# The selective scan's block below the diagonal by way of the states, with one decay tile for both diagonal blocks

## What is computed

```python
value = silu(v_conv)                                   # (B, 256, 16 heads, 16)
Bm = (xm @ B_proj_w).reshape(Bb, L, HS, NS)            # xm (B, 256, 128), NS = 64
Cm = (xm @ C_proj_w).reshape(Bb, L, HS, NS)
decay = exp(A * dt)                                    # one number per head
# chunks of 64 tokens; inside a chunk:
y_diag = einsum('bchqk,bchkp->bchqp', (C B^T) * decay**(q-k), x_dt)
states = einsum('bchtn,bchtp->bchnp', Bp * decay**(chunk-1-t), x_dt)
y_off  = einsum('bchtn,bchnp->bchtp', Cp, h_carry) * decay**(t+1)
y = (y_diag + y_off) + D_param * value
y = y.reshape(Bb, L, DI) * silu(gate) @ out_proj_w
```

## Time and profile before

| | |
|---|---|
| median of 3 runs | 1000.96 us (999.48 to 1003.15) |
| the profiled execution | 1003.44 us |
| its span, first to last instruction | 1001.7 us |
| TensorE | 926.0 us busy, 92% of the span |
| VectorE | 668.7 us, 67% |
| ScalarE | 647.6 us, 65% |
| GpSimd | 463.9 us, 46% |
| mean granted TensorE clock | 0.991 |

### The profile page before, as it was taken

How to read it: one execution, slowest core, us unless ns; L and a number is a source line. 1 busy time by engine, 2 the same in 40 slices (tenths; PEclk the granted TensorE clock), 3 DMA queues, 4 the chain that set the end, 5 groups by cost and what they waited for, 6 DMA issues and landing times.

```text
span 1001.7 us, 24912 instructions
## 1 busy us (share of the span) xinstructions
PE 926.0 (92%) x9520; PEld 802.7 (80%) x9520; DVE 668.7 (67%) x1962; ACT 647.6 (65%) x1511; POOL 463.9 (46%) x739
## 2 busy tenths in 40 slices
PE   6879989898999999999999999999999999999996
PEld 6768778676978888796978879797988877878896
DVE  5345888987867676867668577767768685753320
ACT  3664636767658576776668577676767678578541
POOL 2385333536263644626265344725354447355432
PEclk9999999999999999999999999999999999999999
DMA  7000000000000000000000000000000000000000
GB/s 275 1 2 7 12 7 2 7 3 11 2 18 1 2 18 6 13 2 17 2 17 2 2 17 2 17 2 17 2 17 2 8 7 11 1 13 12 12 6 6
DMA packets 17204, 14.47 MB, mean 14 GB/s; under 512 B 1856, under 2 KB 15552, under 8 KB 16832
## 3 DMA queue, kind: packets, MB, share of 16 engines
q1 hardware_dynamic: 17088, 12.89, 4.1%
HBM read 10.79 MB, written 2.10 MB: 13 GB/s over the span
## 4 chain that ended last, share of the span: by engine, by line
PE 58%; ACT 14%; DVE 11%; POOL 10%; issue 6%; DMA 0%; SPq 0%; POOLq 0%; ACTq 0%; DVEq 0%
PE bank L1239 54%; DVE M L1030 3%; POOL hD_lo L647 3%; POOL P L577 2%; ACT h L890 2%; POOL hD_lo L642 2%; ACT P L857 2%; PE bank L1250 2%; DVE mneg L1148 1%; ACT h L896 1%; DVE cv L1017 1%; POOL w_h_lo L634 1%; ACT junk L698 1%; ACT LM L692 1%; ACT L890 1%
## 5 line engine op out<-in xcount | busy, mean ns | idle before, releaser
L1030 DVE TENSOR_TENSOR M<-bank,LM 128x384 f32<-128x384 f32 x256 | 126.4, 549 | 69.4 <-PE bank L1239 69.3
L1239 PE MATMUL bank<-hD_hi,w_h_hi 128*128 128x256 f32 x512 | 147.7, 288 | 8.9 <-POOL hD_lo L647 6.5
L1239 PE MATMUL bank<-hD_hi,w_h_lo 128*128 128x256 f32 x512 | 143.6, 280 | 0.0
L1239 PE MATMUL bank<-hD_lo,w_h_hi 128*128 128x256 f32 x512 | 143.5, 280 | 0.0
L1148 DVE TENSOR_REDUCE mneg<-bank 128x2 f32<-128x512 f32 (+1 forms) x192 | 122.1, 683 | 13.7 <-PE bank L1239 13.5
L857 ACT ACTIVATE P<-bank 128x512 f32<-128x512 f32 x192 | 102.7, 611 | 18.2 <-PE bank L1239 18.0
L577 POOL TENSOR_SCALAR_AFFINE_SELECT P<-P 128x256 f32<-128x256 f32 (+1 forms) x192 | 91.5, 495 | 36.8 <-ACT P L857 34.1
L1239 PEld LDWEIGHTS bank<-hD_hi,w_h_hi 128*128 128x128 f32 x512 | 96.5, 188 | 13.8 <-POOL hD_lo L647 9.3
L1239 PE MATMUL bank<-BC 64*128 64x256 f32 (+1 forms) x1024 | 101.5, 337 | 4.8 <-ACT BC L705 3.6
L705 ACT ACTIVATE BC<-bank 128x512 f32<-128x512 f32 x128 | 75.3, 606 | 46.3 <-PE bank L1239 43.7
L896 ACT ACTIVATE h<-bank,cols 128x256 f32<-128x256 f32 x128 | 53.4, 471 | 79.3 <-PE bank L1239 78.9
(11 more groups left out here) (252 smaller groups left out, 2643.4 us busy)
## 6 DMA issues: line engine op xcount, KB each, us to landing
xh<-in_x SPq DMA_DIRECT2D x16, 128.0 KB, 2.1
P<-in_w_h SPq DMA_DIRECT2D x2, 1024.0 KB, 9.0
x_res<-in_x SPq DMA_DIRECT2D x16, 128.0 KB, 2.4
out<-out_sb SPq DMA_DIRECT2D x16, 128.0 KB, 1.9
M<-in_w_B SPq DMA_DIRECT2D x1, 512.0 KB, 3.9
M<-in_w_C SPq DMA_DIRECT2D x1, 512.0 KB, 4.4
Qs<-in_w SPq DMA_DIRECT2D x2, 256.0 KB, 5.3
M<-in_w_in SPq DMA_DIRECT2D x1, 256.0 KB, 3.1
```

Source lines behind the costliest of these rows:

```text
L1030: last = v.tensor_tensor(M[:, k % 2, r, e, :], psum("C", i, 2 * n + e)[:, 0:TRI], LM[:, h + e, :, :].rearrange("p a q -> p (a q)"), ALU.mult)
L1239: return p.matmul(o, lhsT, rhs, start=start, stop=True, skip_group_check=True)
```

## The change

The block below the diagonal is no longer made as a 128 x 128 product for each head. The values of the first tile are scaled by decay^(127-k) (`xw`, on DVE), multiplied by `xm` (`gs`, one fp32 product with 256 columns), copied by ACT (`Gs`), and turned into the states of all heads by eight fp32 products with `w_B` as the stationary operand and 32 columns each (`st`); DVE keeps each head's own part (`Sp`). In `va`, four more products of 128 columns take `Sp` times C of the second tile into a bank of their own; DVE multiplies that by decay^(q+1) (`yo`), and POOL adds it (`yadd`). `LM` keeps one 128 x 128 block per head, which serves both diagonal blocks. `sc` makes eight products of 128 columns for four heads and holds two banks; `mask` becomes one DVE operation of 128 x 512 for two heads and two tiles. `BC` gets eight tiles, so that all C of a unit stay until `va`. `w_B` gets a tile of its own. `TURNS`, `BANKS` and `FILL` are new: 220 identity products, 94 in unit 0, 15 in unit 1, 79 in the last two units, 32 in the units between (54 before). In unit 0 TensorE's order is now `bc` 0, `bc` 1, `sc` 0, `bc` 2, `bc` 3, `sc` 1, `gs`, `bc` 4, `st`, then four items of unit 1; DVE takes `st` ahead of its first two `mask` items, and ACT takes the first `bc` after one of the four groups of exponentials, where it took it after all four.

```diff
-    xm_hi=1, n_hi=1, conv=2 * KC, val=1, cb_full=SCORES, masked=SCORES, y_mm=2, yacc_free=2, yg=2,
+    xm_hi=1, n_hi=1, conv=2 * KC, val=1, xw=1, cb_full=4, masked=8, y_mm=2, yo=2, yacc_free=2, yadd=2, yg=2,
...
-    LM = sb("LM", [P, HS, 3, P])
+    LM = sb("LM", [P, HS, P])
+    DR = sb("DR", [P, HS])
+    DQ = sb("DQ", [P, 2, P])
...
         def yg_(i, b):
+            late = yg[:, b, P:L]
+            pool.wait_ge(S["yo"], at(i, "yo", b + 1))
             pool.wait_ge(S["yacc_free"], at(i, "yacc_free", b + 1))
+            g.tensor_tensor(late, late, yo[:, b, :], ALU.add).then_inc(S["yadd"], 1)
+            pool.wait_ge(S["yadd"], at(i, "yadd", b + 1))
             g.tensor_tensor(yg[:, b, :], yg[:, b, :], gate[:, b, :], ALU.mult).then_inc(S["yg"], 1)
...
             for h in range(4 * k, 4 * k + 4):
-                last = a.activation(LM[:, h, :, :].rearrange("p a q -> p (a q)"), diff, ACT.Exp, scale=sc[:, 3, h:h + 1])
+                last = a.activation(LM[:, h, :], diff, ACT.Exp, scale=sc[:, 3, h:h + 1])
+            if k == 0:
+                a.activation(DR[:], sc[:, 3, 0:HS], ACT.Exp, scale=back)
+                for b in range(2):
+                    last = a.activation(DQ[:, b, :], steps, ACT.Exp, scale=sc[:, 3, HS + b:HS + b + 1])
...
         def bc(i, hp):
-            if SCORES * i + hp >= 4:
-                act.wait_ge(S["cb_full"], at(i, "cb_full", hp - 3))
-            copy("S", i, hp, BC[hp % 4][:].rearrange("p m l -> p (m l)"))
+            if i > 0:
+                act.wait_ge(S["y_mm"], at(i, "y_mm", hp // 4 - 1))
+            copy("S", i, hp, BC[hp][:].rearrange("p m l -> p (m l)"))
+
+        def gs_(i, _):
+            if i > 0:
+                wait_full(act, "M", i - 1, M_ST)
+            copy("M", i, M_GS, Gs[:], psum_t("M", i, M_GS))
...
+        def xw_(i, _):
...
+            v.tensor_tensor(xw[:].rearrange("p (b h c) -> p b h c", b=2, c=PS), first, left, ALU.mult).then_inc(S["xw"], 1)
+
+        def st_(i, _):
...
+            wait_full(dve, "M", i, M_ST)
+            of = psum_t("M", i, M_ST).rearrange("p (n c) -> p n c", c=2 * PS)
+            v.tensor_tensor(Sp[:], of, pairs.unsqueeze(1).to_broadcast([P, SCORES, 2 * PS]), ALU.mult).then_inc(evac("M", M_ST), 1)
...
-            for e in range(2):
-                last = v.tensor_tensor(M[:, k % 2, r, e, :], psum("C", i, 2 * n + e)[:, 0:TRI], LM[:, h + e, :, :].rearrange("p a q -> p (a q)"), ALU.mult)
-            last.then_inc(S["masked"], 1)
...
+            decay = LM[:, h:h + 3:2, :].unsqueeze(2).to_broadcast([P, 2, TILES, P])
+            v.tensor_tensor(M[:, k, e, :, :, :], psum("C", i, n).rearrange("p (n k q) -> p n k q", n=2, q=P), decay, ALU.mult).then_inc(S["masked"], 1)
 
         def yg_(i, b):
             dve.wait_ge(S["y_mm"], at(i, "y_mm", b + 1))
+            if i > 0:
+                dve.wait_ge(S["yadd"], at(i, "yadd", b - 1))
+            v.tensor_tensor(yo[:, b, :], psum("Y", i, 2)[:, b * P:(b + 1) * P], DQ[:, b, :], ALU.mult).then_inc(S["yo"], 1)
...
+        def gs_(i, _):
+            pe.wait_ge(S["xw"], i + 1)
+            wait_free(pe, "M", i, M_GS)
+            mm(psum_t("M", i, M_GS), xm[i % 2][:, 0, :], xw[:], True).then_inc(full("M"), 1)
+
+        def st_(i, _):
+            wait_evac(pe, "M", i, M_GS)
+            wait_free(pe, "M", i, M_ST)
+            for n in range(SCORES):
+                two = slice(2 * PS * n, 2 * PS * (n + 1))
+                last = mm(psum("M", i, M_ST)[:, two], w_B[:, n * P:(n + 1) * P], Gs[:, two], n == 0)
+            last.then_inc(full("M"), 1)
...
-            for n in (2 * k, 2 * k + 1):
-                CB, Bt, Ct = [psum("C", i, 2 * n + e) for e in range(2)], BC[n % 4][:, 0, :], BC[n % 4][:, 1, :]
-                for e in range(2):
-                    r64 = slice(e * NS, (e + 1) * NS)
-                    mm(apart(CB[e][:, 0:TRI]), Bt[r64, 0:P], Ct[r64, 0:L].rearrange("p (a q) -> p a q", q=P), True)
-                for e in range(2):
-                    r64 = slice(e * NS, (e + 1) * NS)
-                    last = mm(CB[e][:, P:L], Bt[r64, P:L], Ct[r64, P:L], False)
-                last.then_inc(S["cb_full"], 1)
+            for e in range(2):
+                wait_free(pe, "C", i, 2 * k + e)
+            for n in range(2):
+                Bt, Ct = [BC[2 * k + n][:, m, :] for m in range(2)]
+                for t in range(TILES):
+                    for e in range(2):
+                        r64, tok, o = slice(e * NS, (e + 1) * NS), slice(t * P, (t + 1) * P), psum("C", i, 2 * k + e)
+                        last = mm(o[:, (TILES * n + t) * P:(TILES * n + t + 1) * P], Bt[r64, tok], Ct[r64, tok], n + t == 0)
+            last.then_inc(S["cb_full"], 1)
...
+            for t in range(TILES):
+                for e in range(2):
+                    for q in range(4):
+                        o = acc[32 * q:32 * q + 32, t * P:(t + 1) * P]
+                        mm(o, xpad[:, t, 8 * b + 2 * q + e, :], M[:, q // 2, e, q % 2, t, :], start=(b + t + e == 0))
+            for q in range(4):
+                last = mm(late[32 * q:32 * q + 32, :], Sp[:, 4 * b + q, :], BC[4 * b + q][:, 1, P:L], start=(b == 0))
```

More of the change, by code:

```diff
@@ L83, in _scan @@
         if k % 2 == 1:
-            items += [("va", k // 2)]
-    return items + [("yg", 1)]
+            items += [("va", k // 2), ("yg", k // 2)]
+    return items
 def _chains():
@@ L185, in _opened @@
     return dict(
-        xm_turn=["M", M_XM], n_turn=["M", M_N], gates=["M", M_G + k], val_turn=["M", M_XT], bc=["S", k], sc=["C"] + [4 * k + h for h in range(4)],
-        va=["Y", 0] if k == 0 else [], m_out=["D", D_O] if k == 0 else [], n2_turn=["D", D_N2], up=["D", D_FC + k],
+        xm_turn=["M", M_XM], n_turn=["M", M_N], gates=["M", M_G + k], val_turn=["M", M_XT], gs=["M", M_GS], st=["M", M_ST], bc=["S", k], sc=["C", 2 * k, 2 * k + 1],
+        va=["Y", 0, 2] if k == 0 else [], m_out=["D", D_O] if k == 0 else [], n2_turn=["D", D_N2], up=["D", D_FC + k],
         down=["Y", 1] if k == 0 else [], n3_turn=["H", H_N3], qkv=["H", H_QKV], qk_turn=["K", K_Q + k], k_turn=["A", A_K],
@@ L230, in program @@
     sl = sb("sl", [P, 512])
-    diff = sl[:, 0:3 * P]
+    diff, steps, back = sl[:, 0:P], sl[:, P:2 * P], sl[:, 2 * P:2 * P + 1]
     sq = sb("sq", [P, TILES, QK, PA])
@@ L293, in program @@
     xpad = sb("xpad", [P, TILES, HS, 2 * PS])
-    BC = [sb(f"BC{b}", [P, 2, L]) for b in range(4)]
-    M = sb("M", [P, 2, 2, 2, TRI])
+    BC = [sb(f"BC{b}", [P, 2, L]) for b in range(SCORES)]
+    M = sb("M", [P, 2, 2, 2, 2, P])
+    xw = sb("xw", [P, DI])
+    Gs = sb("Gs", [P, DI])
+    Sp = sb("Sp", [P, SCORES, 2 * PS])
+    yo = sb("yo", [P, 2, P])
     yg = val
@@ L1334, in va @@
                 wait_evac(pe, "M", i, M_XT)
+                wait_evac(pe, "M", i, M_ST)
                 wait_free(pe, "Y", i, 0)
+                wait_free(pe, "Y", i, 2)
             acc = block(psum("Y", i, 0), b)
+            late = psum("Y", i, 2)[:, b * P:(b + 1) * P]
             pe.wait_ge(S["masked"], at(i, "masked", 4 * b + 4))
-            for k in range(2):
-                for j in range(4):
-                    o = acc[32 * j:32 * j + 32, :].rearrange("p (a q) -> p a q", q=P)
-                    mm(o, xpad[:, 0, 8 * b + 4 * k + j, :], apart(M[:, k, j // 2, j % 2, :]), start=(b + k == 0))
-            for k in range(2):
-                for j in range(4):
-                    last = mm(acc[32 * j:32 * j + 32, P:L], xpad[:, 1, 8 * b + 4 * k + j, :], M[:, k, j // 2, j % 2, P:L], False)
+            for t in range(TILES):
[5 more added lines that the diff above has]
+                last = mm(late[32 * q:32 * q + 32, :], Sp[:, 4 * b + q, :], BC[4 * b + q][:, 1, P:L], start=(b == 0))
             last.then_inc(S["y_mm"], 1)
```

196 lines of the change are left out of this document (99 added, 97 removed).

## The result

The changed kernel takes 1022.8 us (median of 4 runs, 1022.1 to 1024.8) against 1002.0 (999.5 to 1003.2) for the kernel before beside it: a ratio of 1.022, 95% interval 1.020 to 1.024. It is slower by 20.8 us, where 992 was forecast with a range up to 1011. The profiled execution has a span of 1021.2 us against 1001.7.

The account below looks back on a forecast made before the run. TensorE, 96% busy from 250 to 800 us, was taken as the bound: 1003.44 - 1.6 (work) - 4 (start) - 4 (idle later) = 993.8 us profiled, median 991.4, stated as 992, range 975 to 1011.

Parts of the forecast that it names:

- The states cost TensorE what the triangle saves: TensorE's work: columns saved in sc and va are paid back in st's weight loads; sum with fills -1.6 us.
- four terms: TensorE's product changes over the run: sc -28.2 us, va -7.0, gs +7.0, st +29.8.
- Fills: -3.2 us: TensorE's identity products: 220 for 232 at 0.27 us each, counted as 3.2 us less work.
- has fewer holes: Units 1 to 13: fills placed in TensorE's idle time go from 77 to 47, read as a sign of fewer holes.
- The start: -4 us: Start of the run: sc 0 at 33 to 34 us, 3.5 us sooner; net -4 us, bounds 0 and -8.
- the sign named was before 57: Start of the run: val's product by the gate was to come before 57 us; it stood at 59.43.
- whatever else is late there stays: Start of the run: the other causes of TensorE's 20.5 us idle in the first 100 us remain as they were.
- Idle time later: -4 us: TensorE between 100 and 800 us: 4 us of the 12.7 + 23.2 us idle given back, bounds -14 and +8.
- VectorE falls by 30 us: VectorE's busy time: masks from 140 to 87 us, new items add 23; off the path where TensorE is 96% busy.
- `st` lets the clock fall: Rival: each unit's st brings a clock fall of 1.7 us, 27 us in all, 1019 us; chance 0.08.
- the loads of `st` lie bare: Rival: st's weight loads are not covered by streams, +26 us on the sum, 1018 us; chance 0.09.
- even* rival: Rival: work and idle time stay even, the start's gain eaten by its own longer chain; 999 us, chance 0.26.

Follow-up runs that it names:

- experiment 4: Kernel before without the block below the diagonal in sc, masks and va (left out of the output): 975.3 us, ratio 0.975.
- experiment 5: Kernel after without the states (xw, gs, st, Sp, late products, yo, yadd), GpSimd's w_h_lo pieces still long: 982.6 us, ratio 0.983.
- experiment 6: Kernel after without the states (xw, gs, st, Sp, late products, yo, yadd), w_h_lo made in narrow pieces of 128 x 256: 977.5 us, ratio 0.977.
- Experiment 8: Kernel before without the identity products of units 1 to 13 (77 of 232): 1004.0 us, ratio 1.004.
- experiment 1: Kernel after with GpSimd's two w_h_lo subtractions of 128 x 2048 cut into 16 of 128 x 256: 1015.9 us, ratio 1.016.
- experiment 7: Kernel of experiment 1, TensorE reading always-ready tiles in place of xw, Gs and Sp, which are still made: 1013.3 us, ratio 1.013.
- experiment 3: Kernel after with st in one fp32r pass for two, 8 records for 16: 1009.6 us, ratio 1.010.
- experiment 11: Kernel of experiment 1 with GpSimd's 64 hD_lo subtractions replaced by writes of zeros: 1001.7 us, ratio 1.000.

## Why the prediction was wrong

**"The states cost TensorE what the triangle saves"** was right on the products that it priced, and 2.8 us off. From start to start, summed over the run without idle time: `sc` 97.2 to 72.2 us, -25.0 (predicted -28.2); `va` with the late products 46.1 to 39.8, -6.3 (-7.0); `gs` +7.9 (+7.0); `st` +27.8 (+29.8). That is +4.4, where the same four terms made +1.6. The pace taken for `st`, that of a load, was the right one: 1.70 us for 16 records. The term that was mis-sized most is `sc`: its groups take 72.2 / 64 = 1.13 us on average for the 1.08 of the sum. In time the two did not balance: the states cost 38.4 us and the triangle had cost 24.9 (experiments 4 to 6), since TensorE waits more where products are taken out.

**4.1 us more of products** (8.5 - 4.4) belong to no step of the prediction. Some 3 of them are the hidden layer's products (`hD` with `w_h`, 1536 records), which go from 187.6 to 190.7 us, start to start. They rose without the states too (190.6 and 189.2 in experiments 5 and 6), and not in experiment 4 (187.6). Neither the states nor `st` is the cause; what is was not settled.

**"Fills: -3.2 us" is the first step that failed.** It counted fewer identity products as work saved. Experiment 8 shows that they are not such a term: 21.6 us fewer made the kernel 3.5 us slower. The same error stood in the sign that the order "has fewer holes": 47 products for 77 in the middle need not mean fewer waits; without the states the holes are the same in both orders (148.1 and 148.5). Between 250 and 800 us TensorE's busy time fell by 8.6 us while its identity products became fewer.

**"The start: -4 us" is the second.** Its first link was right: `sc` 0 at 33.5 us for 36.95. But by unit 0's `m_out` the gain of 3.4 us was gone or nearly so, at 58.8 us against 60.3, where the sign named was before 57. Without the states the same order has it at 54.4 (experiment 5), so the longer chain of unit 0 costs 4.4 us where the prediction had 1.5; TensorE's idle time in the first 60 us is 15.9 us for 16.8. And "whatever else is late there stays" was taken for granted. What VectorE does between 62 and 72 us was new: the conv of unit 1 now met `w_h_lo`. That cost a wait of 8.2 us on TensorE and 5 to 7 us of time (experiment 1), more than the start had won. Both halves of it could have been read beforehand, in the diff and in the trace: the order of VectorE's items, and two GpSimd operations of 4.6 us with two SBUF inputs. The prediction priced VectorE's items by their quiet durations and never asked what ran beside them.

**"Idle time later: -4 us" is the third.** No such gain came. From 250 to 800 us TensorE is idle for 31.8 us, where it was for 23.2. Without the collision the kernel has holes of 143.7 us against 139.0. Of these 4.7 us, 2.6 are put down to the three hand-overs (experiment 7, within its noise); about 2 stay open. Taking work from TensorE does not by itself close holes, it opens some: without the triangle (experiment 4) products fell by 37.6 us and holes grew by 9.1.

**"VectorE falls by 30 us"** was wrong too, though it is off the path. The row of masks fell as forecast for each, 683 ns for 128 x 512, from 126.4 to 82.8 us in the row:

```profile
L1059 DVE TENSOR_TENSOR M<-bank,LM 128x512 f32<-128x512 f32 x128 | 82.8, 683 | 19.2 <-PE bank L1270 18.8
...
L1029 DVE SCALAR_TENSOR_TENSOR cv<-vpad,cols,cv 128x256 f32<-128x256 f32 x96 | 67.3, 701 | 3.4
...
L1065 DVE TENSOR_TENSOR yo<-bank,DQ 128x128 f32<-128x128 f32 x32 | 8.9, 278 | 13.0 <-PE bank L1270 13.0
L1046 DVE TENSOR_TENSOR Sp<-bank,cols 128x256 f32<-128x256 f32 x16 | 6.8, 425 | 51.1 <-PE bank L1270 51.1
L1039 DVE TENSOR_TENSOR xw<-bank,DR 128x256 f32<-128x256 f32 x16 | 6.7, 421 | 14.7 <-PE bank L1332 13.1 <-ACT DQ L699 1.6
```

The prediction took 256 x 549 = 140 us for the old masks, where overlapping ones are busy for 126.4, and 87 for the new. It had them fall by 53 us, and they fell by 43.6: that is 9 of the 38 us missing. The added items cost what was said, 8.9 + 6.8 + 6.7 = 22.4 us. The `cv` row grew by 17 us, from 50.0 (521 ns each) to 67.3 (701), without one `cv` more: hold-ups by GpSimd. It falls to 60.2 with the narrow pieces and to 51.7 when GpSimd writes zeros for `hD_lo` as well (experiments 1 and 11). The other 12 us are spread over small rows.

**The rivals.** That `st` lets the clock fall did not happen: 0.989 for 0.991, and 0.002 of 1021 us is 2.0 us at most. The clock of the kernel after falls at 60, 70, 312, 456 and 848 us, each time over 20 us behind the last `st`; the longest fall (0.51 on the mean from 70 to 77 us) is where TensorE comes out of the collision's wait of 8.2 us. That the loads of `st` lie bare did not happen either. The forecast missed upward by neither of the two mechanisms it had put there. Of the *even* rival one condition did come true, the start's gain eaten by its own longer chain.

**The sum as it should read**, in spans: +4.4 (the four terms) + 4.1 (slower products elsewhere, of which 3 in the hidden layer) + 6.3 (the collision) + 2.6 (hand-overs, within noise) + 2.1 (open) = 19.5 us. What is shown in it by edits of their own is the collision and that `st`'s records weigh in full (experiment 3); the other terms are read from the traces, and 6.2 us (4.1 and 2.1) stay without a cause. By the medians, the experiments that leave parts out split the whole 20.8 us: 5.2 for the collision, 13.5 for the states in place of the triangle, and 2.2 for the new order itself, to within rounding.

## What to carry to other kernels

When a change gives an engine's queue a new order, the durations in the trace of before hold only with their old neighbours: list the long GpSimd operations that read SBUF, and look at which VectorE operations with all their tensors in SBUF the new order puts beside them; cutting such an operation into pieces cost GpSimd 2.4 us here and gave the kernel 5 to 7. It is no rule for every operation: halving the 64 of 1.29 us, for whose results TensorE waits, cost 7.5 us. Identity products that keep TensorE busy in its waits belong with the idle time, not with the work. And where TensorE sets the pace, an exchange of one product for another pays only by a clear difference of their prices on TensorE: the work it dropped gave back 25 to 28 us for 37.6 of products, and the work it took on cost 38 for 43.4.

## What the runs showed of the hardware that was not expected

A VectorE operation of 485 ns lasted 4.64 us beside a GpSimd operation of 4.63, both with two inputs from SBUF; one with an input from a bank was not held. Two inputs are not needed for it: the first step of a conv reads one tensor of SBUF, takes 0.41 us, and lasted 1.48 beside two `hD_lo` in the kernel after:

```profile
L1026 DVE TENSOR_SCALAR cv<-vpad,cols x32: 402/411/1477, 20.9 to 786.4; 128x256 f32<-128x256 f32 x32
```

Products with 128 columns of weights and a stream of 32 columns follow each other at 0.11 us a record, the same pace as with a stream of 128. And 77 identity products of 0.28 us, put where TensorE would otherwise wait, were worth 3.5 us of 1000 (granted clock 0.984 without them, 0.991 with them), though they compute nothing.
